# Attention's value projection in split float32r products, and the output's bias products moved ahead of the heads' products

## The chip, the cores and the metric

One Trainium2 chip, one of its cores. The metric is the device time of one execution in microseconds (us), the median of several. The kernel before took 234.5 us.

## The reference, cut to what matters

Four graph layers run one after another on 128 nodes with 512 features. The change is in the first, an attention layer over a dense 128 by 128 mask:

```python
q = (x @ Wq + bq).reshape(N, H, HEAD)          # N = 128, H = 8, HEAD = 64
k = (x @ Wk + bk).reshape(N, H, HEAD)
v = (x @ Wv + bv).reshape(N, H, HEAD)          # the values: x is 128x512, Wv 512x512
scores = jnp.einsum('nhd,mhd->nhm', q, k) / np.sqrt(HEAD)
scores = jnp.where(adj[:, None, :] == 0, -1000000000.0, scores)
attn = jax.nn.softmax(scores, axis=1)          # over the heads
attn_out = jnp.einsum('nhm,mhd->nhd', attn, v).reshape(N, D_OUT)
attn_out = attn_out @ Wo + bo
h1 = _layer_norm(x + attn_out, g1, be1)
```

After it come a feed-forward block, an edge layer over 4096 edges (which holds most of the time), a graph convolution and a last linear layer.

## The kernel before, in words

The kernel is written by engine: each engine has one list of instructions in a fixed order, and semaphores tie the lists together. No planner moves anything; what stands behind a wait in a list waits too.

Products in plain float32 run slowly on TensorE. For most large products the kernel therefore splits each operand into a high part, which is the operand written as float32r, and a remainder, operand minus high part, also float32r. Then it adds three products: high by high, remainder by high, high by remainder. High parts are made by ScalarE copies and remainders by VectorE subtractions. The queries, keys and values still use plain float32 products.

The order around the change:

- SyncE issues the loads in the order x, Wq, Wk, Wv (L249), edge attributes, Wo, and so on.
- VectorE copies the transposed x from PSUM to `xT` (L995), builds two bf16 one-hot tiles for counting edges (L1001), makes the bias parts (L1011, L1013) and `Wclo` (L1025), and then runs the softmax over the heads: two maxima read from PSUM (L1027, L1028), their maximum (L1029, both inputs in SBUF), the subtraction from the scores (L1031, one input in PSUM), the sums over heads (L1036, L1038, L1039, both inputs in SBUF), the reciprocal (L1040), the mask (L1042) and the scaling of the attention weights (L1044), in two halves. After that it makes the remainders of Wo (`wo_low`, L1048) and of the attention's output (L1053).
- ScalarE makes the bias parts' first step (L345), the column biases (L347), qT and kT (L351 and L356, through the helper at L342), `Wchi` (L353), then waits for the edge counts: `CTs` (L386), `uniform` (L388), the two exponentials (L391). It waits for the values in PSUM (`v_done`), copies them to SBUF (L394), makes the four high parts of Wo (L397), and waits for the heads' products (`ao_done`) to make their high parts (L400).
- TensorE does q, k, the scores (L612), the edge counts (L605), the values (L620: 4 products of 128x512 in float32, recorded as 8 matmuls) with their bias (L622), the transposes of edge attributes (L559), then waits for the values in SBUF: `uniform` by values (L629), the heads' products (L633, each half of them after its half of the attention weights), the two bias products of the output (L637), and the output product in three split parts (L642, L646, L649, through the helper at L535).
- GpSimd does four small instructions for constants at the start, and then only nine inverse roots on 128x1 columns (L320), the first of them for the first layer norm, long after the attention.

The wait that separates values and attention is this:

```python
pe.wait_ge(S["wv_in"], 16)
for c in range(KC):
    mm(bank[3][:, :], xT[:, c, :], Wv[:, c, :], start=c == 0, stop=False)
```

Of the kernel before, what the change touches and what calls it, by code (L numbers as in the profile page):

```python
# [4 lines left out]
F32 = mybir.dt.float32  # L5
F32R = mybir.dt.float32r
BF16 = mybir.dt.bfloat16
I32 = mybir.dt.int32
ALU = mybir.AluOpType
ACT = mybir.ActivationFunctionType  # L10
# [4 lines left out]
D = 512  # L15
KC = D // P
# [19 lines left out]
def tile_of(g, i):  # L36

    return 2 * GT * (g // 2) + 2 * i + g % 2


def gnn_kernel(nc, a, out):

    ctx = ExitStack()
    with ctx:
        def sb(name, shape, dt=F32):
            return ctx.enter_context(nc.sbuf_tensor(name, shape, dt))

        def sem(name):
            return ctx.enter_context(nc.semaphore(name))
# [5 lines left out]
        xT = sb("xT", [P, KC, N])  # L55
# [22 lines left out]
        ones2 = sb("ones2", [2, N], F32R)  # L78
# [5 lines left out]
        def overlay(*spots):  # L84

            made = {}
            with ExitStack() as st:
                end = 0
                for name, place, units, dt in sorted(spots, key=lambda s: s[1]):
                    if place > end:  # L90
                        st.enter_context(nc.sbuf_tensor(f"gap{place}_{name}", [P, (place - end) * D], F32))
                    words = units * D * (2 if dt == BF16 else 1)
                    made[name] = st.enter_context(nc.sbuf_tensor(name, [P, words], dt))[:, :]
                    end = place + units
            return made
# [19 lines left out]

        loop_ids = overlay(("src_ids", 73, 8, I32), ("dst_ids0", 81, 4, I32), ("dst_ids1", 91, 4, I32))

        wo_split = overlay(("Wohi", 32, 4, F32R), ("aoThi", 48, 1, F32R), ("aoTlo", 49, 1, F32R), ("Wolo", 60, 4, F32R))
        ctx.enter_context(nc.sbuf_tensor("region", [P, 95 * D], F32))

        bvo, bvo_parts = thin["bvo"][0:2, :], thin["bvo_parts"][0:2, :]

        def chunks(v, k):
            return v.rearrange("p (c n) -> p c n", c=k)

        Wq, Wk, Wv, Wo, W2raw = (chunks(first[n], KC) for n in ("Wq", "Wk", "Wv", "Wo", "W2raw"))
        F1, F2, ffT, W1raw = chunks(first["F1"], KC), chunks(first["F2"], FC), chunks(first["ffT"], FC), chunks(first["W1raw"], 2 * KC)
        qT, kT = (chunks(first["MA"][:, i * D:(i + 1) * D], KC) for i in (0, 1))
        Wohi, Wolo, aoThi, aoTlo = (chunks(wo_split[n], KC) for n in ("Wohi", "Wolo", "aoThi", "aoTlo"))
        v_sb = first["MA"][:, 2 * D:3 * D]  # L130
        attn = first["attn"].rearrange("p (o j n) -> p o j n", o=2, j=KC)
        ea, Wc, Wchi, Wclo = chunks(first["ea"], ET), first["Wc"], first["Wchi"], other["Wclo"]
# [3 lines left out]
        xhi, xlo = chunks(other["xhi"], KC), chunks(other["xlo"], KC)  # L136
# [29 lines left out]
        bank = [ctx.enter_context(nc.psum_tensor(f"bank{i}", [P, D], F32)) for i in range(8)]  # L166
# [3 lines left out]
        O_BANKS = (bank[5], bank[6])  # L170
# [3 lines left out]
        def quarter(b, j):  # L174
            return b[:, P * j:P * (j + 1)]

        def flat(v):
            return v.rearrange("p c n -> p (c n)")
# [23 lines left out]
            return s - 2 if s in (8, 9, 11) else s - 1  # L202

        S = {}
        for name in ("x_in warm_ready ids_in row_ids_in0 row_ids_in1 dst_ids_in0 dst_ids_in1 loop_src_in loop_dst_in oh_ready st_ready vecs_in ea_in wq_in0 wq_in1 wq_in2 wq_in3 wk_in0 wk_in1 wk_in2 wk_in3 ids_twice wv_in wo_in f1_in f2_in w1_in wc_in w2_in w3_in w4_in g_in ws_in wn_in b1g_in "
                     "out_stored consts ident_ready x_transposed xT_ready cols_done cols_ready q_done k_done v_done "
                     "qk_ready v_ready onehot_bf ct_done ct_read uniform_ready eighth ea_done ea_hi ea_lo wc_hi wc_lo bvo_in bvo_hi bvo_parts sign_ready scores_done s_centred exp_done attn_ready ao_done ao_hi ao_lo wo_hi wo_lo wo_done "
                     "stat_ready rstd_ready nx_ready nT_done nT_ready f1_done ff_ready f2_done pre_done pre_read late_done late_read "
                     "xw_ready w2_hi w2_lo w1_hi w1_lo xs_hi xs_lo ab_done ab_ready "
                     "graphT_ready graphT_done graph_ready deg_ready dinv_ready "  # L210
                     "z1_done z1_read h_hi h_lo z2_done z2_read m_hi m_lo m_oh agg_done "
                     "agg_ready aggT_done aggT_ready u_done u_ready o_done "
                     "ones_ready sum_done sum_ready y2_ready y2T_done y2T_ready z_done r0_ready g_done g_ready g3_done nm_done l3_done w4_hi w4_lo u_hi u_lo last_hi last_lo xl_hi xl_lo nm_hi nm_lo wt_turned xb_ready diag_ready w_out cn_scaled s_done s_scaled centred y_centred y_final0 y_final1 "
                     "late_rows_in dve_chain").split():
            S[name] = sem(name)
# [92 lines left out]
        @block.gpsimd  # L308
        def _(pool):
            pool.iota(iota_row[:, :], pattern=[[1, P]], base=0, channel_multiplier=0,  # L310
                      allow_small_or_imprecise_dtypes=True).then_inc(S["consts"], 1)
            pool.iota(iota_col[:, :], pattern=[[0, 1]], base=0, channel_multiplier=1,
                      allow_small_or_imprecise_dtypes=True).then_inc(S["consts"], 1)
            pool.memset(mhalf[:, :], -0.5).then_inc(S["consts"], 1)
            pool.memset(eighth[:, :], 1.0 / HEADS).then_inc(S["eighth"], 1)
            pool.wait_ge(S["consts"], 3)

            def inverse_root(k, src, dst, ready, signal):
                pool.wait_ge(ready, k)
                pool.tensor_tensor(dst, src, mhalf[:, :], ALU.pow).then_inc(signal, 1)  # L320

            for n in range(8):
                inverse_root(n + 1, mv[:, 1:2], rstd[:, n:n + 1], S["stat_ready"], S["rstd_ready"])
                if n == 0:
                    inverse_root(1, small[:, 1:2], small[:, 2:3], S["deg_ready"], S["dinv_ready"])
# [3 lines left out]
        def _(act):  # L329
# [11 lines left out]
            def bias_out(dst, src, name, j, func=ACT.Identity):  # L341
                return act.activation(dst, src, func, bias=cols[:, col[name] + j:col[name] + j + 1])  # L342

            act.wait_ge(S["bvo_in"], 32)
            act.activation(bvo_parts, bvo, ACT.Copy).then_inc(S["bvo_hi"], 1)  # L345
            act.wait_ge(S["cols_done"], 1)
# [7 lines left out]
            for j in range(KC):  # L354
                act.wait_ge(S["k_done"], j // 2 + 1)
                bias_out(kT[:, j, :], quarter(bank[3 + j // 2], j), "L0_gnn_bk", j).then_inc(S["qk_ready"], 1)  # L356

            def edge_term_out(steps):

                for s in steps:  # L360
                    q, j = s // KC, s % KC
                    for o in range(2):
                        k = 2 * s + o
                        src = step_banks(s)[o]
                        if s < RING_STEPS:
                            act.wait_ge(S["pre_done"], k + 1)
                            signal = "pre_read"
                        else:
                            act.wait_ge(S["late_done"], k - 2 * RING_STEPS + 1)
                            signal = "late_read"  # L370
                        bias_out(C[:, 2 * q + o, j, :], src[:, :], "L1_gnn_b1", j).then_inc(S[signal], 1)
# [138 lines left out]
        def _(pe):  # L510
            mm = nc.tensor.matmul
# [43 lines left out]
            def turn_features(q):  # L555

                for i in range(GT):
                    t = tile_of(2 * q, i)
                    done = nc.tensor.transpose(quarter(EA_BANKS[q], i), flat(ea[:, t:t + 2, :]), ident[:, :])  # L559
                done.then_inc(S["ea_done"], 1)  # L560
# [54 lines left out]
            count_edges(range(ET)).then_inc(S["ct_done"], 1)  # L615


            pe.wait_ge(S["wv_in"], 16)
            for c in range(KC):
                mm(bank[3][:, :], xT[:, c, :], Wv[:, c, :], start=c == 0, stop=False)  # L620
            pe.wait_ge(S["bvo_parts"], 1)
            mm(bank[3][:, :], ones2[:, :], bvo_parts[:, 0:D], start=False, stop=True).then_inc(S["v_done"], 1)  # L622
            pe.wait_ge(S["ea_in"], 16)
            turn_features(0)

            pe.wait_ge(S["v_ready"], 1)
            pe.wait_ge(S["uniform_ready"], 1)
# [2 lines left out]
            for o, j in ((o, j) for o in range(2) for j in range(KC)):  # L630
# [2 lines left out]
                done = mm(bank[3][HEAD * o:HEAD * (o + 1), P * j:P * (j + 1)], v_sb[:, HEAD * h:HEAD * (h + 1)], attn[:, o, j, :],  # L633
                          start=False, stop=j == KC - 1)
            done.then_inc(S["ao_done"], 1)
            for b in range(2):
                mm(O_BANKS[b][:, 0:D // 2], ones2[:, :], bvo_parts[:, D + D // 2 * b:D + D // 2 * (b + 1)], start=False, stop=False)  # L637
            for h in range(2):
                pe.wait_ge(S["ao_hi"], h + 1)
                pe.wait_ge(S["wo_hi"], 2 * (h + 1))  # L640
# [696 lines left out]
```

## Time and profile before

| what | value |
| --- | --- |
| runs | 234.5, 234.52, 235.0 us; median 234.52 |
| the profiled execution | 235.3 us |
| its span in the profile | 232.4 us |
| TensorE busy | 222.9 us, 96% of the span |
| VectorE busy | 176.1 us, 76% |
| ScalarE busy | 127.1 us, 55% |
| GpSimd busy | 5.5 us, 2% (17 instructions) |
| chain that ended last | TensorE 92% of it, ScalarE 3% |

The span is the part of the execution that the engines' records cover; 2.9 us of the profiled execution lie around it. All starts below are counted from the start of the span. A row of the timeline gives start, duration, engine, line, operation, output and inputs, how many, and in brackets the idle time of the engine before it and what ended it. A row of the chain gives start, duration and what held the end of the kernel at that time.

### The profile page before, as it was taken

How to read it: one execution, taken by the hardware profiler on the slowest of the kernel's cores; microseconds unless marked ns; L12 is line 12 of the kernel's file. 1: busy time of each engine (PE TensorE's matmuls, PEld its weight loads, DVE VectorE, ACT ScalarE, POOL GpSimd, SP SyncE). 2: the span in 40 equal slices, each digit the busy share in tenths (PEclk: the TensorE clock that was granted, in tenths of full speed). 3: DMA queues.
4: the chain of work that ended last, by engine and by line, in shares of the span. 5: the costliest groups of instructions: out<-in, count | busy, mean ns of one | idle time of the engine just before them, and what ended most of it. 6: DMA issues, size and time to landing. Idle time of an engine off the chain costs nothing.

```text
span 232.4 us, 3302 instructions
## 1 busy us (share of the span) xinstructions
PE 222.9 (96%) x1212; PEld 181.1 (78%) x1212; DVE 176.1 (76%) x318; ACT 127.1 (55%) x236; POOL 5.5 (2%) x17
## 2 busy tenths in 40 slices
PE   8999999999999999999999999999999999999970
PEld 4985789766766887888888888888888888997860
DVE  2979776767697689875976868878879767987564
ACT  0646489449679636635546646447476544732320
POOL 1000010000000000000000000000000000001001
PEclk9999999999999999999999999999999999999997
DMA  6999999985003927136100000058840000000001
GB/s 219 323 406 395 394 387 405 404 342 185 0 0 127 400 48 119 31 52 110 21 1 3 0 0 1 0 192 315 283 161 0 0 3 1 0 3 0 0 0 45
DMA packets 28614, 31.25 MB, mean 134 GB/s; under 512 B 17948, under 2 KB 18868, under 8 KB 27576
## 3 DMA queue, kind: packets, MB, share of 16 engines
q1 hardware_dynamic: 27808, 30.54, 38.7%
q10 hardware_dynamic: 792, 0.51, 0.8%
q8 instruction: 9, 0.15, 0.3%
q14 instruction: 5, 0.04, 0.1%
HBM read 30.79 MB, written 0.26 MB: 134 GB/s over the span
## 4 chain that ended last, share of the span: by engine, by line
PE 92%; ACT 3%; DVE 1%; issue 1%; POOLq 0%; POOL 0%; DVEq 0%; ACTq 0%
PE bank L745 37%; PE bank L728 13%; PE bank L544 6%; PE bank L535 6%; PE bank L576 4%; PE bank L593 3%; PE bank L755 3%; PE bank L756 3%; ACT C L342 3%; PE bank L620 2%; PE bank L886 1%; PE bank L553 1%; PE bank L704 1%; PE bank L605 1%; PE bank L705 1%
## 5 line engine op out<-in xcount | busy, mean ns | idle before, releaser
L745 PE MATMUL bank<-W2hi,Hhi 128*128 128x512 f32 x128 | 49.8, 389 | 0.0
L745 PE MATMUL bank<-W2hi,Clo 128*128 128x512 f32 x128 | 49.8, 389 | 0.0
L745 PE MATMUL bank<-W2lo,Hhi 128*128 128x512 f32 x128 | 49.8, 389 | 0.0
L435 ACT ACTIVATE Mhi<-M 128x512 fp32r<-128x512 f32 x32 | 20.3, 633 | 44.2 <-DVE M L1142 44.2
L1147 DVE TENSOR_TENSOR Mlo<-M,Mhi 128x512 fp32r<-128x512 f32 x32 | 22.1, 690 | 11.8 <-ACT M L436 11.8
L1142 DVE TENSOR_TENSOR M<-bank,b2r 128x512 f32<-128x512 f32 x32 | 22.0, 687 | 9.5 <-PE bank L756 5.4
L745 PEld LDWEIGHTS bank<-W2hi,Clo 128*128 128x128 f32 x128 | 24.0, 188 | 5.0
L745 PEld LDWEIGHTS bank<-W2hi,Hhi 128*128 128x128 f32 x128 | 24.0, 188 | 5.0
L745 PEld LDWEIGHTS bank<-W2lo,Hhi 128*128 128x128 f32 x128 | 24.0, 188 | 5.0
L428 ACT ACTIVATE Hhi<-C 128x512 fp32r<-128x512 f32 x32 | 20.0, 624 | 11.4 <-DVE C L1128 11.1
L342 ACT ACTIVATE C<-bank,cols 128x512 f32<-128x512 f32 x32 | 19.5, 704 | 10.5 <-PE bank L576 10.5
L1133 DVE TENSOR_TENSOR Clo<-C,Hhi 128x512 fp32r<-128x512 f32 x32 | 22.0, 687 | 3.7 <-ACT C L429 3.7
L1128 DVE TENSOR_TENSOR C<-bank,C 128x512 f32<-128x512 f32 x32 | 21.4, 688 | 3.7 <-PE bank L728 2.7
L728 PE MATMUL bank<-ST,AB 128*128 128x512 f32 x64 | 20.0, 399 | 0.0
L429 ACT ACTIVATE C<-C 128x512 f32<-128x512 f32 x32 | 19.8, 618 | 0.0
L436 ACT ACTIVATE M<-M 128x512 f32<-128x512 f32 x32 | 19.7, 615 | 0.0
L728 PE MATMUL bank<-DT,AB 128*128 128x512 f32 x64 | 19.4, 390 | 0.0
L728 PEld LDWEIGHTS bank<-ST,AB 128*128 128x128 f32 x64 | 11.6, 188 | 3.9 <-DVE C L1128 1.0
L728 PEld LDWEIGHTS bank<-DT,AB 128*128 128x128 f32 x64 | 12.0, 188 | 2.6
L755 PE MATMUL bank<-Mhi,Dg 128*128 128x512 f32 x32 | 12.6, 395 | 0.0
L756 PE MATMUL bank<-Mlo,Dg 128*128 128x512 f32 x32 | 12.5, 389 | 0.0
L320 POOL TENSOR_TENSOR rstd<-mv,mhalf 128x1 f32<-128x1 f32 x8 | 4.4, 548 | 219.2 <-DVE mv L1275 156.5
(253 smaller groups left out, 337.8 us busy)
## 6 DMA issues: line engine op xcount, KB each, us to landing
F<-in_L_gnn_W SPq DMA_DIRECT2D x2, 2048.0 KB, 19.3
W<-in_L_gnn_W SPq DMA_DIRECT2D x3, 1024.0 KB, 5.4
W1raw<-in_L_gnn_W SPq DMA_DIRECT2D x1, 2048.0 KB, 22.4
ids<-in_src SPq DMA_DIRECT2D x2, 1024.0 KB, 13.0
ids<-in_dst SPq DMA_DIRECT2D x2, 1024.0 KB, 7.1
dst_ids<-in_dst SPq DMA_DIRECT2D x2, 1024.0 KB, 7.6
src_ids<-in_src SPq DMA_DIRECT2D x1, 2048.0 KB, 8.4
Wq<-in_L_gnn_Wq SPq DMA_DIRECT2D x4, 256.0 KB, 3.9
```

The lines of the kernel that those rows point to most:

```text
L342: return act.activation(dst, src, func, bias=cols[:, col[name] + j:col[name] + j + 1])
L428: act.activation(Hhi[:, g % 2, j, :], C[:, g, j, :], ACT.Mish)
L429: act.activation(C[:, g, j, :], C[:, g, j, :], ACT.Mish).then_inc(S["h_hi"], 1)
L435: act.activation(Mhi[:, t, :], M[:, t, :], ACT.Mish)
L436: act.activation(M[:, t, :], M[:, t, :], ACT.Mish).then_inc(S["m_hi"], 1)
L728: done = mm(ST1[u % 3][:, :], w[:, P * j:P * (j + 1)], x[:, GE * g:GE * (g + 1)], start=k == 0, stop=k == len(terms) - 1)
L745: done = mm(ST2[t][:, :], x[:, c, e], w[:, c, :], start=c == 0 and i == 0, stop=c == KC - 1 and i == 2)
L755: mm(AGG[:, :], Dg[:, t, :], Mhi[:, t, :], start=g == 0 and t == 0, stop=False)
L1128: v.tensor_tensor(C[:, g, j, :], ST1[u % 3][:, :], C[:, g, j, :], ALU.add).then_inc(S["z1_read"], 1)
L1133: v.tensor_tensor(Hlo[:, g, j, :], C[:, g, j, :], Hhi[:, g % 2, j, :].bitcast(F32), ALU.subtract).then_inc(S["h_lo"], 1)
L1142: v.tensor_tensor(M[:, t, :], ST2[t][:, :], row["L1_gnn_b2"], ALU.add).then_inc(S["z2_read"], 1)
L1147: v.tensor_tensor(Mlo[:, t, :], M[:, t, :], Mhi[:, t, :].bitcast(F32), ALU.subtract).then_inc(S["m_lo"], 1)
```

## The change

The value product becomes three split products. ScalarE makes the high parts of x and of the four row blocks of Wv. GpSimd makes the remainders: one subtraction of 128x512 for x, four of 128x512 for Wv. `Wvlo` is written over Wv, `Wvhi` into a place of its own, `xhi` and `xlo` into places that a later stage uses for the same purpose. TensorE waits for the high parts and, block by block, for the remainders. The two bias products of the output move from behind the heads' products to a place ahead of them, before the wait for the values in SBUF.

```diff
+        wv_split = overlay(("Wvlo", 8, 4, F32R), ("Wvhi", 12, 4, F32R))
...
@@ GpSimd, after its constants and ahead of the inverse roots
+            pool.wait_ge(S["split_hi"], 1)
+            pool.tensor_tensor(flat(xlo), flat(xT[:, :, :]), flat(xhi).bitcast(F32), ALU.subtract).then_inc(S["split_lo"], 1)
+            for c in range(KC):
+                pool.wait_ge(S["split_hi"], c + 2)
+                pool.tensor_tensor(Wvlo[:, c, :], Wv[:, c, :], Wvhi[:, c, :].bitcast(F32), ALU.subtract).then_inc(S["split_lo"], 1)
@@ ScalarE, ahead of the bias parts (L344)
+            act.wait_ge(S["xT_ready"], 1)
+            act.activation(flat(xhi), flat(xT[:, :, :]), ACT.Copy).then_inc(S["split_hi"], 1)
@@ ScalarE, behind kT (L356) and ahead of the wait for the edge counts (L385)
+            act.wait_ge(S["wv_in"], 16)
+            for c in range(KC):
+                act.activation(Wvhi[:, c, :], Wv[:, c, :], ACT.Copy).then_inc(S["split_hi"], 1)
@@ TensorE, L618
-            pe.wait_ge(S["wv_in"], 16)
+            pe.wait_ge(S["split_hi"], KC + 1)
             for c in range(KC):
-                mm(bank[3][:, :], xT[:, c, :], Wv[:, c, :], start=c == 0, stop=False)
+                mm(bank[3][:, :], xhi[:, c, :], Wvhi[:, c, :], start=c == 0, stop=False)
+            pe.wait_ge(S["split_lo"], 1)
+            for c in range(KC):
+                mm(bank[3][:, :], xlo[:, c, :], Wvhi[:, c, :], start=False, stop=False)
+            for c in range(KC):
+                pe.wait_ge(S["split_lo"], c + 2)
+                mm(bank[3][:, :], xhi[:, c, :], Wvlo[:, c, :], start=False, stop=False)
             pe.wait_ge(S["bvo_parts"], 1)
             mm(bank[3][:, :], ones2[:, :], bvo_parts[:, 0:D], start=False, stop=True).then_inc(S["v_done"], 1)
             pe.wait_ge(S["ea_in"], 16)
             turn_features(0)
+            for b in range(2):
+                mm(O_BANKS[b][:, 0:D // 2], ones2[:, :], bvo_parts[:, D + D // 2 * b:D + D // 2 * (b + 1)], start=False, stop=False)
 
             pe.wait_ge(S["v_ready"], 1)
@@ TensorE, L636, behind the heads' products
-            for b in range(2):
-                mm(O_BANKS[b][:, 0:D // 2], ones2[:, :], bvo_parts[:, D + D // 2 * b:D + D // 2 * (b + 1)], start=False, stop=False)
```

## Rows read from the trace of the kernel before

**Rows 1.** The chain that ended last, in order of time: start, us, what.

```profile
16.54 3.49 PE bank L620 x8
20.03 0.44 PE bank L622
...
20.50 0.61 ACT MA L394
...
21.15 1.16 PE bank L629 x8
22.30 1.52 PE bank L633 x16
...
23.85 0.67 ACT aoThi L400 x2
```

**Rows 2.** The same chain in the edge layer, sixty split products of 128x512.

```profile
73.77 13.63 PE bank L745 x60
```

**Rows 3.** Timeline of ScalarE, 9 to 24 us.

```profile
9.64 0.19 ACT L347 ACTIVATE cols<-bank 128x24 f32<-128x24 f32 x1 [1.25 <-PE bank L600]
...
12.97 1.14 ACT L342 ACTIVATE MA<-bank,cols 128x128 f32<-128x128 f32 x4 [0.57 <-PE bank L593]
16.58 0.28 ACT L386 ACTIVATE CTs<-bank 128x128 f32<-128x128 f32 x1 [2.47 <-PE bank L605]
...
20.99 2.18 ACT L397 ACTIVATE Wohi<-Wo 128x512 fp32r<-128x512 f32 x4
```

**Rows 4.** The load of Wv, line 249: its issue, and from issue to landing.

```profile
L249 SPq DMA_DIRECT2D Wv<-in_L_gnn_Wv x1: 466/466/466, 5.0 to 5.0; - x1
...
DMA to landing us min/median/max: 9.2/9.2/9.2
```

**Rows 5.** Timeline of GpSimd, whole span.

```profile
0.83 0.24 POOL L310 IOTA iota_row<- 128x128 f32 x1 [0.39 <-POOLq L1327]
1.02 0.14 POOL L312 IOTA iota_col<- 128x1 f32 x1
...
33.40 0.55 POOL L320 TENSOR_TENSOR small<-small,mhalf 128x1 f32<-128x1 f32 x1 [4.11 <-DVE small L1065]
50.06 0.55 POOL L320 TENSOR_TENSOR rstd<-mv,mhalf 128x1 f32<-128x1 f32 x1 [16.11 <-DVE mv L970]
```

**Rows 6.** Timeline of VectorE, the softmax, 14 to 24 us.

```profile
14.70 0.69 DVE L1027 TENSOR_REDUCE y<-bank 128x128 f32<-128x512 f32 x1 [1.58 <-PE bank L612]
...
16.02 0.29 DVE L1029 TENSOR_TENSOR total<-y 128x128 f32<-128x128 f32 x1
16.35 1.29 DVE L1031 TENSOR_TENSOR attn<-bank,total 128x512 f32<-128x512 f32 x2
17.73 0.42 DVE L1036 TENSOR_TENSOR y<-attn 128x256 f32<-128x256 f32 x1
18.20 0.29 DVE L1038 TENSOR_TENSOR y<-y 128x128 f32<-128x128 f32 x1
...
20.95 1.29 DVE L1044 TENSOR_TENSOR attn<-attn,total 128x512 f32<-128x512 f32 x2
22.16 1.29 DVE L1048 TENSOR_TENSOR Wolo<-Wo,Wohi 128x512 fp32r<-128x512 f32 x2
```

**Rows 7.** Timeline of VectorE beside two of GpSimd's inverse roots.

```profile
33.82 0.29 DVE L1069 TENSOR_TENSOR mask<-CTs,ident 128x128 f32<-128x128 f32 x1
34.48 0.29 DVE L1071 TENSOR_SCALAR Ahat<-mask,small 128x128 f32<-128x128 f32 x1 [0.38 <-DVE mask L1069]
...
50.02 0.77 DVE L979 SCALAR_TENSOR_TENSOR y<-y,mv,rows 128x512 f32<-128x512 f32 x1
50.83 0.75 DVE L982 SCALAR_TENSOR_TENSOR y<-y,rstd,rows 128x512 f32<-128x512 f32 x1
```

**Rows 8.** Timeline of TensorE and its weight loads, 20 to 25 us.

```profile
20.39 0.66 PE L559 MATMUL bank<-ident,ea 128*128 128x128 f32 x4
...
23.75 0.29 PEld L637 LDWEIGHTS bank<-bvo_parts,ones 2*128 2x128 f32 x2 [0.17 <-issue]
...
24.29 1.22 PE L535 MATMUL bank<-Wohi,aoThi 128*128 128x256 f32 x8
```

**Rows 9.** Timeline of VectorE, second half of the feed-forward block's output.

```profile
48.83 0.42 DVE L947 TENSOR_TENSOR y<-bank,xw 128x256 f32<-128x256 f32 x1 [1.63 <-PE bank L535]
```

More of the change, by code:

```diff
@@ L129, in gnn_kernel @@
         Wohi, Wolo, aoThi, aoTlo = (chunks(wo_split[n], KC) for n in ("Wohi", "Wolo", "aoThi", "aoTlo"))
+        Wvhi, Wvlo = (chunks(wv_split[n], KC) for n in ("Wvhi", "Wvlo"))
         v_sb = first["MA"][:, 2 * D:3 * D]
@@ L204, in gnn_kernel @@
         S = {}
-        for name in ("x_in warm_ready ids_in row_ids_in0 row_ids_in1 dst_ids_in0 dst_ids_in1 loop_src_in loop_dst_in oh_ready st_ready vecs_in ea_in wq_in0 wq_in1 wq_in2 wq_in3 wk_in0 wk_in1 wk_in2 wk_in3 ids_twice wv_in wo_in f1_in f2_in w1_in wc_in w2_in w3_in w4_in g_in ws_in wn_in b1g_in "
+        for name in ("x_in warm_ready ids_in row_ids_in0 row_ids_in1 dst_ids_in0 dst_ids_in1 loop_src_in loop_dst_in oh_ready st_ready vecs_in ea_in wq_in0 wq_in1 wq_in2 wq_in3 wk_in0 wk_in1 wk_in2 wk_in3 ids_twice wv_in wo_in f1_in f2_in w1_in wc_in w2_in w3_in w4_in g_in ws_in wn_in split_hi split_lo b1g_in "
                      "out_stored consts ident_ready x_transposed xT_ready cols_done cols_ready q_done k_done v_done "
```

## The prediction

> **What bounds the kernel now.** I read the table of busy shares first: TensorE is busy for 96% of the span, and it holds 92% of the chain that ended last. Then I followed that chain through the attention. From 16.54 to 20.48 us it lies on the value products and their bias, then on ScalarE's copy of the values, then on the uniform and heads' products, and from 23.85 on ScalarE's high parts of the result [rows 1]. So the value products are on the path. The question is how close other paths run. VectorE's softmax gives the first half of the attention weights at 20.95 + 0.66 = 21.61 us and the second at 22.24 [rows 6], while the heads' products start at 22.30 and reach their second half at 22.30 + 0.76 = 23.06 [rows 1]. The softmax thus trails the path by only 0.69 us (first half) and 0.82 us (second).
>
> A gain or a loss at the heads' products carries through to the end. The output product's remainder half of Wo comes from VectorE behind them. The one place where a fixed arrival could swallow it is the feed-forward block; there VectorE still waits 1.63 us for TensorE [rows 9], and after it the chain is TensorE or what TensorE releases.
>
> **The products themselves.** Four float32 products take 3.49 us [rows 1]. A split product of the same 128x512 takes 13.63 / 60 = 0.227 us [rows 2], so twelve take 2.73 us: 0.76 us less, if nothing is waited for.
>
> **ScalarE.** The high part of x costs one copy of 128x512. Wo's four copies take 2.18 us with a last one of 0.62, a pitch of 0.52 [rows 3]. ScalarE idles 1.25 us before the column biases [rows 3], and 0.52 fits in; without that idle time q would come later by it. The four copies of Wv go where ScalarE idles 2.47 us before the edge counts [rows 3]. Wv is issued at 5.0 and lands 9.2 us later, at about 14.2 [rows 4], and kT is done at 14.11 [rows 3]. The high parts come at about 14.86, 15.38, 15.90 and 16.42. TensorE is free at 16.54 and the edge counts are read at 16.58, so this costs nothing, with 0.1 us to spare. Queued behind this new wait are the edge counts, `uniform` and the exponentials; a Wv landing 0.5 us later would push them all by 0.4 us, of which the softmax's margin hides it.
>
> **GpSimd's subtraction, the unknown size.** The trace shows no GpSimd instruction of this size. The low bound is VectorE's like subtraction, 0.65 us (two in 1.29) [rows 6]. The upper bound is three streams plus the fixed part: GpSimd's iota writes 128 columns in 0.24 us and one in 0.14, so 127 columns cost 0.10 and 512 some 0.40 for one stream; two inputs and one output one after another give 1.20, and with the 0.55 us of the smallest two-input instruction [rows 5] 1.75. With the write beside the reads and the 0.14 once it is 0.95, with all three streams apart 1.35. I take the middle, 1.15 us.
>
> The Trainium skill's page "GPSIMD Engine Reference" (section "Performance versus the Vector engine") gives 4497 ns for an add of 2048 columns; a quarter of it, an estimate by that page, is 1.12 us. No run here shows it yet.
>
> The remainder of x is ready early: it can start at 8 us, and even if it held up VectorE by its whole 1.15, VectorE idles 1.58 us before the softmax [rows 6]. The remainders of Wv start at about 14.95. Unhindered they end at 16.10, 17.25, 18.40 and 19.55. TensorE does its eight products by high parts from 16.54 to 18.36, then must wait for the fourth remainder: 19.55 + 0.05, the product 0.23, the bias 0.44 as now [rows 1], and `v_done` comes at 20.27 in place of 20.47. Of the 0.76 us, 0.2 is left.
>
> **The bias products.** Their weight loads hold the engine 0.29 us [rows 8]. At the old place the next product starts at 24.29 [rows 8], but the high part it needs comes at about 24.2 from ScalarE [rows 1]; taking them away gains at most 0.05. At the new place they follow the transposes, which end about 0.59 us after `v_done`, while the values reach SBUF 0.65 us after it [rows 1, 8]. So the uniform products start 0.23 us later against `v_done` than before. Together: 20.27 + 0.59 + 0.29 = 21.15, the same as now [rows 1]. Without a quarrel over memory the whole change is worth nothing.
>
> **The quarrel, the term that decides.** From 14.95 to 19.55 GpSimd reads two SBUF tiles, just when VectorE's softmax reads two SBUF tiles (L1029, L1036, L1038, L1039) [rows 6]. The trace has two places where both engines are at it. At 33.40 GpSimd begins a root which by its span ends at 33.95, and VectorE, which needs it, starts only at 34.48 after idling 0.38 us behind the mask [rows 5, 7]: about 0.5 us went somewhere while VectorE ran its SBUF instructions. At 50.06 the other root runs beside a two-input instruction, and the next VectorE instruction, which needs the root, follows at once at 50.83; the first took 0.77 against 0.75 [rows 5, 7]. So the rows show a hold-up once, almost none the other time. Bounds for the softmax: nothing, up to all four subtractions in one piece. I take turns, one instruction each, since the place at 33.4, with short VectorE instructions in a row, is the nearest to this one.
>
> Worked out with 1.15 us: the first subtraction ends at 16.10, so L1029 starts 0.08 late and ends at 16.39. L1031 reads PSUM and one tile and doesn't matter; the second subtraction runs 16.39 to 17.54, the third to 18.69. L1036, due at 17.81, starts at 18.69: 0.88. It ends at 19.12, the fourth runs to 20.27, and L1038, due at 19.16, waits 1.11. Sum 2.07 us for the softmax. Less the margin of 0.69 the heads' products are late by **1.38 us**. The values are ready long before (`v_done` 20.27 + 0.72 = 20.99), so nothing more is added.
>
> The Trainium skill has this as a rule: its page "SBUF — State Buffer" (section "SBUF: two separate sides") says that VectorE with two SBUF inputs and a GpSimd instruction that reads SBUF share a port pair as an exclusive lock, held for a whole instruction. By that rule the sum is the 1.38 us above; without it, 0. The trace agrees at 33.4 us and speaks against it at 50.0 us.
>
> **Sum.** Against the profiled execution: 235.3 + 1.4 = 236.7 us (span 233.8). The median of the runs is 0.8 us under the profiled execution, so the forecast for it is 234.5 + 1.4 = 235.9 us.
>
> **The rivals.**
> - *No quarrel, 1.15 us each.* For it: the rows at 50.0 us. Against: those at 33.4. The sum is 0: 234.5 us. A subtraction of 1.35 us moves `v_done` by 0.8 and gives 235.3.
> - *Faster: GpSimd fast enough and undisturbed.* The place is the fourth remainder. At 1.0 us it ends at 18.95, `v_done` comes at 19.67, the uniform products start at 20.55 and end at 21.71, and the heads' products start 0.59 us earlier than now; below that the weights at 21.61 stop it at 0.65. It passes 0.2% from about 1.03 us downwards. For it: the low bound of 0.65 and the 0.95. Against: it needs both no quarrel and a fast engine. 233.9 us.
> - *GpSimd keeps the memory between its instructions.* L1029 waits from 16.02 to 19.55, 3.53 us, less 0.69: +2.8, 237.3 us. Against: GpSimd waits for a semaphore between subtractions.
> - *VectorE first each time*: the fourth subtraction slips to the reciprocal at about 20 to 21 us and `v_done` to about 22: some +2, inside the range.
>
> **How the numbers follow.** A measurement here can tell about 0.2%, 0.47 us, from no change. Turns, in either order or partly shared: 0.55. No quarrel: 0.25, counted as the same. Faster: 0.15. GpSimd in one piece: 0.05. That gives faster 0.15, same 0.25, slower 0.60. The range goes from 234.0, which leaves the faster case out, to 237.3. The slower cases' own range is 235.1 to 237.3.
>
> **What would show it.** Right: GpSimd's four subtractions at a pitch over 1.15 us between 15 and 20.5; gaps of about 1 us before L1036 and L1038's counterparts; the first half of the attention weights at about 23.7; TensorE waiting for the weights, not for the values; value products of 0.227 us each with a gap before the last one. Wrong: a softmax with its old gaps, and TensorE waiting for the values' copy. If the softmax is undisturbed and the pitch is under 1.03 us, the faster case has happened. A late Wv would show as edge counts read after 16.6.

## The result, and the profile after

The changed kernel takes 236.88 us (median of 6 runs, 236.49 to 237.42), the kernel before 235.08 (6 runs): the ratio is 1.008, with an interval of 1.006 to 1.0099, so 1.4 to 2.3 us more. The profiled executions give 234.2 us of span against 232.4. The change made the kernel slower, as forecast; the size forecast, 1.4 us, lies at the lower edge of what was measured. The median of the kernel before is 0.6 us higher over its six runs than over the first three, on which the forecast of 235.9 us was built, so it is the differences that should be compared.

The chain that ended last, in order of time (start, us, what), no longer goes through the value products. It goes through VectorE:

```profile
14.65 0.69 DVE y L1048
...
15.97 0.79 DVE total L1050
...
18.18 1.27 DVE y L1057
...
19.48 1.25 DVE y L1059
...
23.18 0.70 DVE attn L1065
...
23.93 1.70 PE bank L656 x16
...
25.66 0.67 ACT aoThi L415 x2
```

The heads' products begin at 23.93 us; before, they began at 22.30 [rows 1]. The softmax starts where it did, 14.65 against 14.70 [rows 6], so the loss is inside it. VectorE's timeline of the changed kernel names the instructions:

```profile
15.97 0.78 DVE L1050 TENSOR_TENSOR total<-y 128x128 f32<-128x128 f32 x1
16.79 1.29 DVE L1052 TENSOR_TENSOR attn<-bank,total 128x512 f32<-128x512 f32 x2
18.18 1.26 DVE L1057 TENSOR_TENSOR y<-attn 128x256 f32<-128x256 f32 x1
19.48 1.24 DVE L1059 TENSOR_TENSOR y<-y 128x128 f32<-128x128 f32 x1
20.76 0.43 DVE L1057 TENSOR_TENSOR y<-attn 128x256 f32<-128x256 f32 x1
21.22 0.29 DVE L1059 TENSOR_TENSOR y<-y 128x128 f32<-128x128 f32 x1
```

Compare the durations with those before [rows 6]: 0.78 against 0.29, 1.26 against 0.42, 1.24 against 0.29. No idle time stands in brackets. A held-up instruction looks long in the record; it doesn't look late. The two whose inputs come from PSUM and one tile (L1052) kept 1.29 for the pair. After 20.6 us the same lines are back at 0.43 and 0.29. GpSimd's timeline says why:

```profile
8.20 3.15 POOL L323 TENSOR_TENSOR xlo<-xT,xhi 128x512 fp32r<-128x512 f32 x1 [6.97 <-ACT xhi L355]
15.33 5.24 POOL L326 TENSOR_TENSOR Wvlo<-Wv,Wvhi 128x512 fp32r<-128x512 f32 x4 [3.98 <-ACT Wvhi L371]
```

The four subtractions lie from 15.33 to 20.57 us. They start at 15.33, 16.56, 17.88 and 19.12. VectorE's long instructions end one after another just behind theirs: 16.75 behind the first, 19.44 behind the third, 20.72 behind the fourth.

Two more rows of the same kernel, ScalarE's timeline, then TensorE's:

```profile
14.62 2.19 ACT L371 ACTIVATE Wvhi<-Wv 128x512 fp32r<-128x512 f32 x4 [0.56 <-DMA Wv<-in_L_gnn_Wv]
16.72 0.25 ACT L401 ACTIVATE CTs<-bank 128x128 f32<-128x128 f32 x1
```

```profile
16.87 1.19 PE L635 MATMUL bank<-Wvhi,xhi 128*128 128x512 f32 x4 [0.37 <-ACT Wvhi L371]
17.90 1.08 PE L638 MATMUL bank<-Wvhi,xlo 128*128 128x512 f32 x4
18.82 0.90 PE L641 MATMUL bank<-Wvlo,xhi 128*128 128x512 f32 x3
20.63 0.50 PE L641 MATMUL bank<-Wvlo,xhi 128*128 128x512 f32 x1 [0.91 <-POOL Wvlo L326]
22.50 1.16 PE L652 MATMUL bank<-uniform,MA 128*128 128x128 f32 x8
23.93 1.69 PE L656 MATMUL bank<-attn,MA 128*64 128x128 f32 x16 [0.27 <-DVE attn L1065]
26.09 1.21 PE L550 MATMUL bank<-Wohi,aoThi 128*128 128x256 f32 x8 [0.47 <-ACT aoThi L415]
```

TensorE waited 0.91 us for the fourth remainder, then 0.27 us for the attention weights. The values are later too: the uniform products start at 22.50, before at 21.15 [rows 1]. The weights are only 0.27 us behind them. So two paths arrive almost together. With a softmax that nobody holds up, the uniform products would still end about 1.2 to 1.3 us later than before (an estimate: 22.50 against 21.15, less 0.1 us if each of the four subtractions took 1.28).

The first output product starts at 26.09 us, before at 24.29 [rows 8]. That is the whole loss of this execution, 1.80 us. The heads' products start 1.63 us late, and by the chain they take 1.70 us instead of 1.52 [rows 1].

### The profile page after: what moved, and what is told of

Its sections match the earlier page's. It is cut to its first block, busy times and chain, and to the rows that moved or that the text cites. A ratio compares the mean times of both kernels' runs of the same rounds, so it can differ in the third digit from the quotient of the medians.

```text
span 234.2 us, 3320 instructions
## 1 busy us (share of the span) xinstructions
PE 222.8 (95%) x1216; PEld 181.9 (78%) x1216; DVE 179.4 (77%) x318; ACT 129.7 (55%) x241; POOL 13.9 (6%) x22
## 4 chain that ended last, share of the span: by engine, by line
PE 88%; DVE 5%; ACT 3%; issue 1%; POOLq 0%; POOL 0%; DVEq 0%; ACTq 0%
PE bank L766 37%; PE bank L749 13%; PE bank L559 6%; PE bank L550 6%; PE bank L591 4%; PE bank L608 3%; PE bank L776 3%; PE bank L777 3%; ACT C L352 3%; PE bank L907 1%; PE bank L568 1%; PE bank L725 1%; PE bank L726 1%; PE bank L730 1%; PE bank L855 1%
## 5 line engine op out<-in xcount | busy, mean ns | idle before, releaser
L1168 DVE TENSOR_TENSOR Mlo<-M,Mhi 128x512 fp32r<-128x512 f32 x32 | 22.1, 689 | 11.8 <-ACT M L451 11.8
```

The lines of the kernel that those rows point to most:

```text
L1168: v.tensor_tensor(Mlo[:, t, :], M[:, t, :], Mhi[:, t, :].bitcast(F32), ALU.subtract).then_inc(S["m_lo"], 1)
```

## The experiments

The theory: GpSimd and VectorE take turns at SBUF, one instruction each, when both read it as these do; VectorE's softmax loses about 2 us, and 0.69 us of that is hidden. The main rival: TensorE's new waits, or the high parts that come late, make the loss. The kernel before was run beside each group of kernels on the same chip; the intervals are those of the ratio to it.

**Parts of the change alone.** First only the bias products (e1_bias_only):

```diff
 turn_features(0)
+for b in range(2):
+    mm(O_BANKS[b]..., ones2, bvo_parts...)
...
 done.then_inc(S["ao_done"], 1)
-for b in range(2):
-    mm(O_BANKS[b]..., ones2, bvo_parts...)
```

> The kernel before with the two bias products of the output moved ahead of the heads' products, and nothing else. In the trace of before their weight loads take 0.29 us and the values reach SBUF about 0.06 us after the transposes end, so my theory is that the uniform products start about 0.2 us later and the kernel takes 0.1 to 0.2 us more (within 0.2% of before). A rival, that the move fills idle time for nothing and clears the way to the output product, expects 0 to 0.1 us less.

Measured: ratio 1.0022, interval 1.0001 to 1.0042, which holds anything from nothing to 1 us. Its trace tells more. From the softmax's first instruction to the uniform products it is 21.22 - 14.51 = 6.71 us, before 21.15 - 14.70 = 6.45; to ScalarE's high parts of the output 9.41 us, before 9.15. The move costs 0.26 us and gives nothing back. By this trace the rival of a gain falls.

The other part alone is the changed kernel with these products back at their old place (the reverse of the diff above; e2_split_only).

> The changed kernel with the bias products back behind the heads' products. Theory: the heads' products wait for the attention weights, so where the bias products stand is worth nothing: the time of the changed kernel within 0.1 us, about 1.8 us over before. Rival (the move is part of the loss): 0.2 us less than the changed kernel.

Measured: ratio 1.0077, interval 1.0051 to 1.0102, median 237.07 us; the changed kernel has 1.008. The place of the bias products is worth nothing that these runs can tell once the softmax is late. In this profile TensorE's clock fell, which is treated below.

**The remainders taken out of GpSimd** (e3_no_remainders).

```diff
-for c in range(KC):
-    pool.wait_ge(S["split_hi"], c + 2)
-    pool.tensor_tensor(Wvlo[:, c, :], Wv[:, c, :], Wvhi[:, c, :]..., ALU.subtract)...
...
-    pe.wait_ge(S["split_lo"], c + 2)
-    mm(bank[3][:, :], xhi[:, c, :], Wvlo[:, c, :], ...)
+    mm(bank[3][:, :], xhi[:, c, :], Wvhi[:, c, :], ...)
```

> The changed kernel without GpSimd's four subtractions for Wv; TensorE reads the high parts a second time in their place, so the remainder product of Wv is replaced by another of the same size. Everything else of the change stays. Theory (GpSimd and VectorE take turns at SBUF): VectorE's sums go back to 0.29 and 0.42 us, the heads' products start at about 22.1 us, and the kernel takes 0.2 to 0.5 us less than before. Rival (ScalarE's copies, the later Wv or TensorE's new waits cause the loss): 0.5 to 1.8 us more than before remain.

Measured: ratio 0.9998, interval 0.9979 to 1.0016. The loss is gone with the four subtractions. High parts, late Wv and twelve products are all still there, so these parts of the rival fall. But TensorE's wait for the remainders is gone as well, so this run cannot separate that wait from the softmax. (This kernel leaves out the remainder product of Wv and computes other values.) VectorE's sums are back:

```profile
16.08 0.29 DVE L1046 TENSOR_TENSOR total<-y 128x128 f32<-128x128 f32 x1
17.98 0.43 DVE L1053 TENSOR_TENSOR y<-attn 128x256 f32<-128x256 f32 x1 [0.28 <-ACT attn L403]
18.44 0.29 DVE L1055 TENSOR_TENSOR y<-y 128x128 f32<-128x128 f32 x1
```

But the gain of 0.2 to 0.5 us that I expected isn't there either. In its trace Wv lands 9.8 us after its issue; the high products start at 17.06, 0.46 us after the edge counts let TensorE go, and it is 2.98 us from there to the bias. Counted from the softmax's first instruction the bias begins at 5.28 us, before at 5.26: the late start has eaten what the products save. The bias products then add their 0.26 us, and the heads' products start at 22.58, not at the 22.1 that I expected. So even without GpSimd the split is worth about nothing here.

**The subtractions alone, beside the kernel before** (e4_sub_beside). Values stay float32; GpSimd subtracts Wv from itself into a spare place.

```diff
+pool.wait_ge(S["wv_in"], 16)
+for c in range(KC):
+    pool.tensor_tensor(spare[:, c, :], Wv[:, c, :], Wv[:, c, :], ALU.subtract).then_inc(S["spare_done"], 1)
...
 pe.wait_ge(S["s_centred"], 2)
+pe.wait_ge(S["spare_done"], 4)
```

> The kernel before with four subtractions of 128x512 on GpSimd beside the softmax (Wv minus Wv into a spare place, from the landing of Wv on); TensorE waits for them only ahead of the first edge products at about 27 us. Values as before in float32. Theory: VectorE's two-input instructions in SBUF are held up by 2 us or more and the kernel takes 1.4 to 2.2 us more than before. Rival (the loss comes from TensorE waiting for the remainders, not from VectorE): within 0.2 us of before.

Measured: ratio 0.9999, interval 0.9981 to 1.0016. My number was wrong. By the time alone the theory had failed; the timeline of VectorE and GpSimd shows what happened:

```profile
14.85 4.08 POOL L323 TENSOR_TENSOR spare<-Wv 128x512 f32<-128x512 f32 x4 [13.61 <-DMA Wv<-in_L_gnn_Wv]
...
16.42 0.61 DVE L1037 TENSOR_TENSOR total<-y 128x128 f32<-128x128 f32 x1
17.07 1.29 DVE L1039 TENSOR_TENSOR attn<-bank,total 128x512 f32<-128x512 f32 x2
18.45 0.76 DVE L1044 TENSOR_TENSOR y<-attn 128x256 f32<-128x256 f32 x1
19.24 0.29 DVE L1046 TENSOR_TENSOR y<-y 128x128 f32<-128x128 f32 x1
```

Here the subtractions started 0.25 us ahead of the softmax (15.10); in the changed kernel they start 0.68 us behind it. They follow one another every 1.02 us, with no wait for high parts between. They were done at 18.93, so only two of VectorE's instructions met one: 0.32 + 0.34 = 0.66 us lost, just under the 0.69 that is hidden. What the subtractions cost would then be a matter of when they start. That was a new statement and needed a run of its own: the same kernel with one wait more (e5_subs_later).

```diff
 pool.wait_ge(S["wv_in"], 16)
+pool.wait_ge(S["ct_done"], 1)
```

> The same four subtractions beside the kernel before as in the run e4_sub_beside, but started by the end of the edge counts (about 16.6 us) instead of the landing of Wv (14.85 us). Nothing waits for them before the first edge products. Theory (turns of one instruction each): now three of them meet VectorE's sums at 17.7 us and later, VectorE loses 2.5 to 3.5 us and the kernel takes 1.8 to 2.8 us more than before. Rival (TensorE's waits or the late high parts make the loss, and the subtractions cost VectorE only the 0.7 us of e4_sub_beside): within 0.2 us of before.

Measured: ratio 1.0115, interval 1.0073 to 1.0156, median 237.03 against 235.04. Nothing waits for these subtractions before the edge products, TensorE has no new wait for remainders, and a loss as large as that of the whole change is there:

```profile
16.51 4.26 POOL L324 TENSOR_TENSOR spare<-Wv 128x512 f32<-128x512 f32 x4 [15.27 <-PE bank L613]
...
17.52 1.31 DVE L1045 TENSOR_TENSOR y<-attn 128x256 f32<-128x256 f32 x1
18.86 1.01 DVE L1047 TENSOR_TENSOR y<-y 128x128 f32<-128x128 f32 x1
19.91 1.15 DVE L1045 TENSOR_TENSOR y<-attn 128x256 f32<-128x256 f32 x1
...
20.92 1.16 PE L637 MATMUL bank<-uniform,MA 128*128 128x128 f32 x8
23.80 1.69 PE L641 MATMUL bank<-attn,MA 128*64 128x128 f32 x16 [1.72 <-DVE attn L1053]
```

Three of VectorE's instructions lose 0.89, 0.72 and 0.72 us, and TensorE stands 1.72 us before the heads' products. The sum is 2.33 us, a little under the 2.5 to 3.5 expected; the time is in the range. So the start of the subtractions matters, and the hold-up of the softmax alone is enough for the whole loss. That does not make TensorE's wait harmless in the changed kernel, where it ends only 0.27 us earlier than the wait for the weights. The first of the three instructions shows a detail of the turns: by the records it starts at 17.52 and GpSimd's second subtraction at 17.51, and it lost 0.89 us, most of one subtraction.

**What it is about the subtraction.** The same place and start, first with copies, then with fills:

```diff
-pool.tensor_tensor(spare[:, c, :], Wv[:, c, :], Wv[:, c, :], ALU.subtract)
+pool.tensor_copy(spare[:, c, :], Wv[:, c, :])     # copies
+pool.memset(spare[:, c, :], 0.0)                  # fills
```

> As e5_subs_later, but with four copies of 128x512 on GpSimd (one input in SBUF) in place of the subtractions. Theory, if any reading of SBUF by GpSimd takes turns with VectorE: each copy runs at 0.5 to 0.8 us, VectorE loses about 1 to 2 us, the kernel takes 0.5 to 1.5 us more than before. Rival (only two inputs on both sides collide): within 0.2 us of before.

> As e5_subs_later, but with four fills of 128x512 with zero on GpSimd, which read nothing. Theory, by which VectorE's second input and GpSimd's reading collide: VectorE's sums keep their 0.29 and 0.42 us and the time is within 0.2 us of before. Rival (writing collides too): VectorE loses 0.5 us or more.

Measured: copies 1.0009 (0.999 to 1.0028), fills 0.9994 (0.9973 to 1.0014). The fills took 0.53 us each and touched nothing. The copies, 0.61 us at the least, did hold up two of VectorE's instructions, by 0.29 and 0.28 us:

```profile
17.26 2.53 POOL L324 COPY spare<-Wv 128x512 f32<-128x512 f32 x4 [16.02 <-PE bank L613]
...
18.73 0.58 DVE L1047 TENSOR_TENSOR y<-y 128x128 f32<-128x128 f32 x1
19.35 0.71 DVE L1045 TENSOR_TENSOR y<-attn 128x256 f32<-128x256 f32 x1
```

Together 0.57 us, inside the margin, so the time stays. My sum for the copies (1 to 2 us lost by VectorE) was too high: the first was over before VectorE's sums began at 18.27, and the second ended at 18.43 without holding up the first sum (0.43 us). By its number the rival had won; the records show the hold-up that it denied. So one input that GpSimd reads from SBUF is enough for a collision, and writing alone isn't.

**Fewer blocks.** Only two of the four blocks of Wv are split:

```diff
-for c in range(KC):      # high parts, remainders, and the split products
+for c in range(2):
...
+for c in range(2, KC):
+    mm(bank[3][:, :], xT[:, c, :], Wv[:, c, :], start=False, stop=False)
```

> The changed kernel with only the first two row blocks of Wv split (two subtractions on GpSimd instead of four); the other two blocks stay plain float32 products; bias products at their old place. Theory: the two subtractions end at about 17.9 us, ahead of VectorE's sums at 18.2, and hold up only L1029's counterpart by 0.5 us, less than the margin of 0.69. The value products take 0.38 us less than before, so the kernel takes 0 to 0.3 us less than before. Rival (any GpSimd work in this stretch costs about 0.45 us apiece, a quarter of the 1.8 us of four): 0.9 us more than before.

Measured: ratio 1.0014, interval 0.9988 to 1.0039: no loss of 0.9 us, and no gain to be told either. The trace has VectorE held up once (0.74 in place of 0.29), the values' bias at 19.62 instead of 19.96, and heads' products at 22.14 that waited 0.17 us for the weights. In the kept traces of all kernels the softmax starts anywhere from 14.48 to 15.48 us, with the queries' products starting at 5.38 to 6.36, so a gain of 0.15 us is out of reach of this measurement. This is the best version of the idea that I found, and it doesn't beat the kernel before.

**VectorE does the remainders itself.**

```diff
+for c in range(KC):
+    dve.wait_ge(S["split_hi"], c + 2)
+    dve.wait_ge(S["split_lo"], c + 1)
+    v.tensor_tensor(Wvlo[:, c, :], Wv[:, c, :], Wvhi[:, c, :]..., ALU.subtract).then_inc(S["split_lo"], 1)
 chain(v.tensor_tensor(total[:, :], quarter(y, 0), quarter(y, 1), ALU.max))
```

> The changed kernel with the four remainders of Wv made by VectorE, ahead of L1029's counterpart, instead of by GpSimd. Theory: by turns, GpSimd's four subtractions cost VectorE 2.24 us in the changed kernel, nearly the 2.6 us (four of 0.65) that it takes to make them itself; so this kernel takes 1.7 to 2.0 us more than before, the same as the changed kernel within 0.2 us. Rival (GpSimd's slowness as such, its last remainder at 20.6 us, sets the time): here the last remainder comes at 18.6 us, so 0.5 us or more less than the changed kernel.

Measured: ratio 1.0126, interval 1.0103 to 1.0149, median 237.87 against 235.14, so 2.7 us and not 1.7 to 2.0. The four took 3.08 us instead of 2.6, as each waits for the one before through a semaphore (a wait of my own making), and the maximum behind them starts 3.0 us later, counted from the softmax's start. The last remainder came at 19.89, not at 18.6; counted from the softmax's start that is still 1.5 us earlier than in the changed kernel, and TensorE waited 1.70 us for the weights. So here the softmax decides. But the run made the softmax itself 3.0 us later, more than GpSimd did, so it says little about what TensorE's wait for GpSimd's last remainder would cost by itself. No run does.

**The clock, and the changed kernel again.** In the profile of e2_split_only, the split alone, TensorE's granted clock fell. The table by stretches of that kernel (busy time of TensorE, granted clock, share and rate of the DMA engines):

```profile
20.00:22.00 2.00, 1.19 (x5) 1.00 1.02 363
22.00:23.00 1.00, 0.90 (x8) 1.00 1.04 424
23.00:26.00 3.00, 2.87 (x19) 0.50 1.02 406
26.00:27.00 1.00, 1.00 (x8) 0.79 1.04 391
```

From 23 to 26 us it is 0.50, the 1.2 GHz level, behind a stretch of 2 us in which TensorE was busy for 1.19. The heads' products took 2.67 us instead of 1.58. To test it, products without use fill the waits:

```diff
+keep_warm(4, bank[7])    # ahead of the wait for the last remainder
+keep_warm(2, bank[7])    # ahead of the attention weights
+keep_warm(2, bank[7])    # ahead of the output's high parts
```

> The changed kernel with eight bf16 products without use (128x512, 0.23 us each) placed in TensorE's three new waits: four ahead of the last remainder, two ahead of the attention weights, two ahead of the output's high parts. Theory: in some executions of the changed kernel TensorE's clock falls to half in these waits (as in the profile of e2_split_only at 23 to 26.3 us, with a span 1 us longer); with the waits filled no execution shows a mean clock under 0.988 and the median is 0.2 to 0.5 us under the changed kernel run beside it. Rival (the lower clock has nothing to do with the waits): the same share of executions with a mean clock near 0.984 and the same median within 0.2 us.

> The changed kernel again, on the chip of the two others, to compare them with. Both theories: 1.5 to 2.1 us more than before; of its executions, about one in six to one in three with a mean clock near 0.984 and a span near 235.3 us, the rest at 0.988 to 0.995 with spans of 234.0 to 234.7 us.

Measured: with filled waits 1.0065 (1.0046 to 1.0084), median 236.53; the changed kernel beside it 1.01 (1.007 to 1.013), median 237.56, 2.4 us over the kernel before and so more than the 1.5 to 2.1 expected. The medians are 1.0 us apart, more than the 0.2 to 0.5 expected, though the two intervals overlap. Of the six executions of the changed kernel four had a mean clock of 0.982 to 0.984 and spans of 235.4 to 235.5 us, more than the one in three I expected; the other two had 0.99 and 0.994 with 234.1 and 234.6. With filled waits none was under 0.989. The same table for the changed kernel in this second group of runs has the fall in the uniform and heads' products:

```profile
22.00:22.50 0.50, 0.50 (x5) 0.92 1.03 414
22.50:25.50 3.00, 3.00 (x14) 0.50 1.02 407
25.50:26.00 0.50, 0.50 (x8) 0.67 1.04 389
26.00:27.00 1.00, 0.79 (x11) 1.00 1.06 395
```

The mean clock of an execution does not say where its clock fell. Every trace but e9_vector_remainders has a granted clock of 0.90 to 0.98 from 210 to 232 us, the kernel before too (0.96). Only e2_split_only and this one have a fall between 20 and 30 us, and only these two have a mean under 0.988. Counted by that mean, it is 1 of 6 executions in the first group, 3 of 6 without the moved bias products, 4 of 6 here, 1 of 4 in e5_subs_later and 1 of 4 in e9_vector_remainders. It is none of 6 with filled waits, and none of the 68 executions of the kernel before or of the 68 of the other experiments, in whose traces no wait of TensorE from 20 to 26 us is over 0.5 us. So the fall goes with the waits, but they don't force it. The first trace of the changed kernel has the same waits at full clock, and so has that of e9_vector_remainders, with TensorE nearly idle for 2 us:

```profile
20.00:22.00 2.00, 1.37 (x6) 1.00 1.03 395
...
23.50:25.50 2.00, 0.30 (x4) 1.00 1.01 399
```

(The first line is of the changed kernel, the second of e9_vector_remainders.) That filling the waits is what kept the clock up is likely and not proven: with five of twelve executions of the changed kernel affected, none of six can also be chance.

## Why the prediction was right or wrong

**The direction and the mechanism** held. The likeliest case was turns at SBUF between GpSimd and VectorE with TensorE waiting for the weights, and the profile has it, line by line. One of the signs named for it was wrong: I looked for gaps of about 1 us, and the records show long instructions. By that sign the evidence for choosing turns was weaker than I took it to be. At 33.4 us the root took 0.55 us like the other eight, the mask instruction beside it kept its 0.29, and what was lost stands as idle time [rows 5, 7]. That is not how the hold-ups here look. The choice was right, but not for the reason that I read from the rows.

**GpSimd's subtraction**, taken at 1.15 us between 0.65 and 1.75, measured 1.28 for the first in the changed kernel and 1.03 beside the kernel before, where one tile is subtracted from itself. That the middle of such wide bounds came out 0.13 us off is luck.

**The turns.** Forecast 0.08, 0.88 and 1.11, sum 2.07 us. Measured 0.49, 0.84 and 0.95, sum 2.28. The step that was mis-sized most is the start. Wv landed 9.6 us after its issue instead of 9.2 [rows 4], the high parts and with them GpSimd began at 15.33 instead of 14.95, and the first turn fell on L1029's counterpart with 0.49 us in place of 0.08. I had weighed a late Wv only for ScalarE's queue, not for where it puts GpSimd against VectorE. "This costs nothing, with 0.1 us to spare" was wrong as well: the edge counts were read at 16.72 and TensorE's products started 0.37 us late.

**The values** were not "ready long before". By the forecast's own sum (bias done at 20.99) the uniform products would have ended about 0.65 us ahead of the weights; they started at 22.50 instead of 21.87 (20.99 + 0.59 + 0.29), and TensorE waited only 0.27 us for the weights. Half of the 0.63 us is the fourth remainder at 20.57 instead of 20.27; most of the rest is its product, which after the wait took 0.43 us to the bias instead of 0.23. The values were 0.27 us from setting the time themselves.

**The bias products**: 0.23 us forecast, 0.26 in the trace of the run with them alone. Once the weights were late it counted for nothing, as argued.

**What the sum of 1.4 us lacked.** The profiled execution is 1.8 us longer with the granted clock at 1.00 from 20 to 30 us, so the difference is not in the clock there. It is four small terms: 0.21 us more for the turns, less 0.05 for the softmax's earlier start, 0.09 us from the weights to the products that waited for them, and 0.18 us for the heads' products themselves (1.70 instead of 1.52 by the chain). The last two were put at nothing. In TensorE's timeline the heads' products take 1.69 us where they follow a wait (e5_subs_later, e8_two_blocks, e9_vector_remainders too) and 1.58 in the kernel before and in e1_bias_only, where they don't.

The clock comes on top of that. Without the execution of the first group with the mean clock of 0.983 (237.42 us) the median is 236.64, which is 1.56 us over the kernel before; with filled waits it is 1.4 us over, and in the second group, with four of six, 2.4 us. The forecast asked what is late when TensorE waits, but not what the waiting can do to TensorE.

**The rival of no quarrel** was priced at 0 and the rival of a fast GpSimd at a gain. The run without GpSimd's subtractions says that there was no gain to be had: 0.9998. Their one common assumption, that Wv lands at 14.2 us, gave them 0.4 us too much. The price of 0 for no quarrel was wrong too. It rests on remainders every 1.15 us from 14.95. At the measured start of 15.33 and 1.28 us each the fourth comes at about 20.45, and by the profile's own distances the heads' products start at about 23.5, 1.2 us late with nobody held up (an estimate; no run has this case). So a loss of the right size would not by itself have shown the quarrel. VectorE's long instructions and e5_subs_later do.

The rule of the Trainium skill, page "SBUF — State Buffer", section "SBUF: two separate sides", says that a VectorE instruction with two SBUF inputs is shut out by a GpSimd instruction only if that one reads SBUF, and then for the whole instruction. Copies against fills (0.29 and 0.28 us lost, against none) and the ends of the stretched instructions agree with it. What the lost time at 33.4 us of the kernel before was [rows 5, 7] isn't settled by any run; the changed kernel has it too, 0.37 us of idle time in place of 0.38.

## What to carry to other kernels

Work given to GpSimd is not off VectorE's list if both read SBUF at the same time: before moving it, lay the two timelines side by side and count the meetings, because the same four subtractions cost 0.66 us of VectorE's time or 2.3, depending on when they start. Look for VectorE's stretches that read PSUM, and for starts that hang on a load whose landing varies. Then price the next path as well: here TensorE's wait for the last remainder stands only 0.27 us behind the one that set the time, so freeing the softmax alone would have given back little. And when a change makes TensorE wait a few times in a row, reckon with a lower clock in some executions, beside the wait itself.

## What the runs showed of the hardware that I had not expected

- A held-up instruction shows as a longer duration, on both engines. The remainder of x took 3.15 us on GpSimd, from 8.20 to 11.35; VectorE's one-hot instruction ran until 10.23, and 1.12 us were left behind it. In turn a VectorE instruction with a single SBUF input, over 2x128, took 1.23 us where it had taken 0.20:

```profile
7.94 2.29 DVE L1022 TENSOR_TENSOR Sbf<-scol_twice,numbers 128x4096 bf16<-128x4096 bf16 x1
...
10.21 1.23 DVE L1029 TENSOR_SCALAR ones<-iota_row 2x128 fp32r<-2x128 f32 x1
```

  It cost nothing, as VectorE still idled 0.64 us before the softmax.
- GpSimd's fills of 128x512 took 0.53 us each, its copies from 0.61, subtractions of a tile from itself from 1.03, and subtractions of two different tiles with a float32r result from 1.28.
- Two waits of TensorE, 0.24 and 0.92 us, stood ahead of the fall to 1.2 GHz at about 22.5 us in the profile of e11_changed_again. The fall lasted about 3 us. Nearly the same waits, 0.37 and 0.91 us, left the clock at 1.00 in the profile of the changed kernel's first group, and so did 1.72 us in one piece in that of e5_subs_later.
